# Attention scores with 128 instead of 82 stationary columns, and idle products behind the output projection of each second image

## The reference, cut to what matters

```python
B, N, D = x.shape                       # 32, 164, 192
H, d = (N_HEADS, D_HEAD)                # 12, 16
q = (x @ Wq + bq).reshape(B, N, H, d).transpose(0, 2, 1, 3)
k = (x @ Wk + bk).reshape(B, N, H, d).transpose(0, 2, 1, 3)
scores = jnp.einsum('bhqd,bhkd->bhqk', q, k) * SCALE
allowed = jnp.abs(idx[:, None] - idx[None, :]) <= half      # half = 64
scores = jnp.where(allowed[None, None], scores, -jnp.inf)
```

## Time and profile before

| | |
|---|---|
| median of 3 runs | 2442.05 us (2440.94 to 2452.29) |
| the profiled execution's own time | 2410.74 us |
| its span | 2409.0 us |
| TensorE busy | 2301.1 us, 96% of the span |
| VectorE busy | 1878.0 us, 78% |
| ScalarE busy | 1397.2 us, 58% |
| mean granted clock of TensorE | 0.974 of full speed |

### The profile page before, as it was taken

How to read it: one execution, slowest core, us unless ns; L and a number is a source line. 1 busy time by engine, 2 the same in 40 slices (tenths; PEclk the granted TensorE clock), 3 DMA queues, 4 the chain that set the end, 5 groups by cost and what they waited for, 6 DMA issues and landing times.

```text
span 2409.0 us, 48738 instructions
## 1 busy us (share of the span) xinstructions
PE 2301.1 (96%) x19971; PEld 2153.2 (89%) x19971; DVE 1878.0 (78%) x2364; ACT 1397.2 (58%) x1391; POOL 229.8 (10%) x133
## 2 busy tenths in 40 slices
PE   7699989999999889999999999989999999999999
PEld 6466877777777789999999999989999999999999
DVE  8799755666666487766766767689999999999995
ACT  5689113444444554435435344588888888888881
POOL 5522000000000021211211111000000000000000
PEclk9899997999999899999999999999999999999999
DMA  7655131111111100000000000210000000000000
GB/s 238 178 149 152 47 142 34 45 47 44 47 47 44 37 22 27 20 15 26 20 24 19 19 26 24 90 59 23 24 22 23 23 23 23 23 23 23 23 19 10
DMA packets 99326, 115.82 MB, mean 48 GB/s; under 512 B 15271, under 2 KB 90551, under 8 KB 98487
## 3 DMA queue, kind: packets, MB, share of 16 engines
q1 hardware_dynamic: 79087, 89.38, 12.3%
q10 hardware_dynamic: 16520, 14.34, 2.0%
q0 software_dynamic: 3616, 10.54, 1.7%
HBM read 83.36 MB, written 30.86 MB: 47 GB/s over the span
## 4 chain that ended last, share of the span: by engine, by line
PE 64%; issue 0%; DVE 0%
PE spline_acc L1915 27%; PE spline_acc L1888 10%; PE spline_acc L1887 10%; PE spline_acc L1889 10%; PE spline_acc L1909 5%; PE spline_acc L1911 2%; PE spline_xT L764 0%; DVE spline_f L1664 0%; DVE spline_weights_low L1647 0%; DVE spline_x L1734 0%; DVE spline_x L1737 0%
## 5 line engine op out<-in xcount | busy, mean ns | idle before, releaser
L1915 PE MATMUL spline_acc<-spline_weights,spline_f 128*128 128x192 f32 x3936 | 672.2, 328 | 0.0
L1915 PEld LDWEIGHTS spline_acc<-spline_weights,spline_f 128*128 128x128 f32 x3936 | 637.4, 190 | 0.0
L1887 PE MATMUL spline_acc<-spline_f,spline_weights_high 128*128 128x328 f32 x1536 | 480.5, 313 | 2.5 <-DVE spline_weights_low L1647 2.5
L1888 PE MATMUL spline_acc<-spline_f,spline_weights_high 128*128 128x328 f32 x1536 | 481.2, 313 | 0.0
L1889 PE MATMUL spline_acc<-spline_f,spline_weights_low 128*128 128x328 f32 x1536 | 477.7, 311 | 0.0
L1887 PEld LDWEIGHTS spline_acc<-spline_f,spline_weights_high 128*128 128x128 f32 x1536 | 289.1, 188 | 2.8 <-DVE spline_weights_low L1647 2.8
L1889 PEld LDWEIGHTS spline_acc<-spline_f,spline_weights_low 128*128 128x128 f32 x1536 | 289.3, 188 | 0.0
L1888 PEld LDWEIGHTS spline_acc<-spline_f,spline_weights_high 128*128 128x128 f32 x1536 | 289.3, 188 | 0.0
L1909 PE MATMUL spline_acc<-spline_weights_split,spline_f_high 128*128 128x384 f32 x656 | 218.2, 389 | 8.2 <-issue 8.2
L1664 DVE SCALAR_TENSOR_TENSOR spline_f<-spline_front 128x984 fp32r<-128x984 f32 x128 | 145.6, 1178 | 100.2 <-PE spline_acc L1889 94.9
L1021 DVE TENSOR_REDUCE attend_max<-scores_by_query 82x6 f32<-82x876 f32 x128 | 136.3, 1065 | 57.5 <-PE scores_by_query L1352 56.8
(11 more groups left out here) (229 smaller groups left out, 4266.6 us busy)
## 6 DMA issues: line engine op xcount, KB each, us to landing
spline_front<-pos_scr SPq DMA_DIRECT2D x32, 540.0 KB, 4.4
hid_scr<-spline_hid SPq DMA_DIRECT2D x64, 164.0 KB, 1.8
spline_xn<-hid_scr SPq DMA_DIRECT2D x41, 256.0 KB, 3.1
attend_spread<-rec_scr SPq DMA_DIRECT2D x128, 61.5 KB, 2.1
pix_scr<-spline_front SPq DMA_DIRECT2D x32, 225.0 KB, 3.8
spline_weights_raw<-w SPq DMA_DIRECT2D x1, 6144.0 KB, 21.4
spline_weights<-w SPq DMA_DIRECT2D x4, 1536.0 KB, 6.2
spline_x<-h_scr SPq DMA_DIRECT2D x41, 96.0 KB, 1.9
```

The lines of the kernel that those rows point to most:

```text
L1887: nc.tensor.matmul(z, high, x_high, start=start, stop=False)
L1888: nc.tensor.matmul(z, high, x_low, start=False, stop=False)
L1915: last = nc.tensor.matmul(z, f_rest[i][:, cols], w2[:, i, r, :], start=False, stop=stop)
```

## The change

Two things are done. First, the stationary operand of scores, masks and subtracted maxima is widened from 82 (`ROWS`) to 128 (`P`) columns, and the output with it to 128 partitions of PSUM; partitions 82 to 127 are never read. For this `q1`, `k1` and `k2` become views into tiles `wide` with 46 zeroed columns behind them, `piece` and `pick` are made 128 wide, and POOL zeroes the six tails. Second, `keep_going` is called in each pair but the last, in image 1 in front of part 1, which is behind the output projection: 13 products in the first pair, 4 in the others.

```diff
-        self.piecer = sb("window_piece_r", [P, 2, SPAN], F32R)
+        self.piecer = sb("window_piece_r", [P, 2, WINDOW + P], F32R)
-        self.pickr = sb("attend_pick_r", [P, HG, ROWS], F32R)
+        self.pickr = sb("attend_pick_r", [P, HG, P], F32R)
...
-        q1, k1, k2 = ([sb(f"attend_{k}{u}", [P, HG, PT], F32R) for u in range(2)] for k in ("q1_", "k1_", "k2_"))
+        wide = {k: [sb(f"attend_{k}{u}", [P, HG * PT + P - ROWS], F32R) for u in range(2)] for k in ("q1_", "k1_", "k2_")}
+        q1, k1, k2 = ([y[:, 0:HG * PT].rearrange("p (g n) -> p g n", g=HG) for y in wide[k]] for k in ("q1_", "k1_", "k2_"))
...
+            for y in wide["q1_"] + wide["k1_"] + wide["k2_"]:
+                pool.memset(y[:, HG * PT:].bitcast(F32), 0.0).then_inc(zeros_set, 1)
...
-            pool.wait_ge(zeros_set, 6)
+            pool.wait_ge(zeros_set, 12)
...
+            def columns(k, u, r, g, at):
+
+                at += g * PT
+                return wide[k][u][r, at:at + P]
+
...
-                            nc.tensor.matmul(sc[0:ROWS, j, g * SPAN:(g + 1) * SPAN],
-                                             q1[u][r, g, i * TOK + n * ROWS:i * TOK + (n + 1) * ROWS],
+                            nc.tensor.matmul(sc[:, j, g * SPAN:(g + 1) * SPAN],
+                                             columns("q1_", u, r, g, i * TOK + n * ROWS),
...
-                        last = nc.tensor.matmul(to, piecer[r, n, at:at + ROWS], edge, start=False,
+                        last = nc.tensor.matmul(to, piecer[r, n, at:at + P], edge, start=False,
...
-                            nc.tensor.matmul(tp[0:ROWS, j, g * SPAN:(g + 1) * SPAN],
-                                             k[r, g, i * TOK + c * ROWS:i * TOK + (c + 1) * ROWS],
+                            nc.tensor.matmul(tp[:, j, g * SPAN:(g + 1) * SPAN],
+                                             columns(k, u, r, g, i * TOK + c * ROWS),
...
-                        last = nc.tensor.matmul(tp[0:ROWS, j, g * SPAN:(g + 1) * SPAN], pickr[r, g, :],
+                        last = nc.tensor.matmul(tp[:, j, g * SPAN:(g + 1) * SPAN], pickr[r, g, :],
...
+                        if q == 1 and i == 1 and more:
+                            keep_going(13 if first else 4, xb[:, claim(use(t, V[0])), 0:HG * P])
```

More of the change, by code:

```diff
@@ L142, in stage @@
         self.rest_low = sb("attend_rest_low", [P, 1])
-        self.piece = sb("window_piece", [P, 2, SPAN])
+        self.piece = sb("window_piece", [P, 2, WINDOW + P])
         self.mask = sb("window_mask", [P, 2, EDGE])
-        self.pick = sb("attend_pick", [P, HG, ROWS])
+        self.pick = sb("attend_pick", [P, HG, P])
         self.ones_row = sb("attend_ones_row", [P, PT])
@@ L1000, in _ @@
         def _(dve):
-            dve.wait_ge(zeros_set, 6)
+            dve.wait_ge(zeros_set, 12)
             def norm_in(tt, u):
@@ L1247, in _ @@
                 high(k1[0][:, g, :], start(START["K"][g]))
-            act.wait_ge(zeros_set, 6)
+            act.wait_ge(zeros_set, 12)
             for i in range(2):
@@ L1339, in add_mask @@
                         r = slice(32 * row, 32 * row + 32)
-                        of = scores[0:ROWS, bank, 0:SW].rearrange("p (g n) -> p g n", n=SPAN)
+                        of = scores[:, bank, 0:SW].rearrange("p (g n) -> p g n", n=SPAN)
                         if p < 2:
@@ L1360, in keys_scores @@
                 for g in range(HG):
-                    for k in (k1[u], k2[u]):
+                    for k in ("k1_", "k2_"):
                         for j in range(4):
                             r = slice(32 * j, 32 * j + 32)
-                            nc.tensor.matmul(tp[0:ROWS, j, g * SPAN:(g + 1) * SPAN],
-                                             k[r, g, i * TOK + c * ROWS:i * TOK + (c + 1) * ROWS],
+                            nc.tensor.matmul(tp[:, j, g * SPAN:(g + 1) * SPAN],
+                                             columns(k, u, r, g, i * TOK + c * ROWS),
                                              q1[u][r, g, i * TOK + FROM[c]:i * TOK + FROM[c] + SPAN],
-                                             start=(g == 0 and k is k1[u]), stop=False)
+                                             start=(g == 0 and k == "k1_"), stop=False)
                 add_mask(tp, c, [(j, j) for j in range(4)], False)
@@ L1475, in _ @@
             keep_going(48, tp[:, 0, 0:HG * P])
-            pe.wait_ge(zeros_set, 6)
+            pe.wait_ge(zeros_set, 12)
             for j in range(2):
@@ L2049, in layouts @@
         "wo": wo.reshape(P, HG, D),
-        "pick": np.tile(-(row % DH == group).astype(f32)[..., None], (1, 1, ROWS)),
+        "pick": np.tile(-(row % DH == group).astype(f32)[..., None], (1, 1, P)),
         "minus_low": -np.concatenate([row % 32 >= DH, row % 32 >= DH], 1).astype(f32),
@@ L2054, in layouts @@
         "mask": np.tile(np.where(np.stack([mask, mirror], 1), NEG, 0.0).astype(f32), (4, 1, 1)),
-        "piece": np.tile(np.stack([piece, piece[:, ::-1]], 1).astype(f32), (4, 1, 1)),
+        "piece": np.tile(np.pad(np.stack([piece, piece[:, ::-1]], 1), ((0, 0), (0, 0), (0, P - ROWS))).astype(f32), (4, 1, 1)),
         "patches": x.reshape(B, 3, HS, K, HS, K).transpose(1, 3, 5, 0, 2, 4).reshape(PATCH, B, PIX),
```

## The result

The changed kernel took 2475.76 us (median of 6 runs, 2462.14 to 2486.78), the kernel before 2439.78 us (median of its 6 runs, 2412.88 to 2452.29). The ratio is 1.0176, with a 95% interval from 1.0132 to 1.022: slower, by 43 us as the ratio has it (32 to 54) and 36 us by the medians. The two differ because the ratio leaves out the run of 2452.29 us, which is over 1.5% above the fastest of its kernel and so counts as a slow one. I had forecast 22 us, and 2464 us as the time.

The account below looks back on a forecast made before the run. PE was taken to bound attention, busy 26.8 of 29.2 us a pair. Span 2409.0 + 43.3 (wider sets, idle products) - 21.4 (clock) = 2430.9; by medians 2442.05 + 21.9 = 2464 us, range 2432 to 2488.

Parts of the forecast that it names:

- What bounds the kernel, and the step of a set: Attention: PE bounds it; the load sets the step, 0.109 us a set with 128 columns, 0.036 more than before.
- rival 2: Scores and masks in attention: wide loads don't bound the sets, so the kernel gets faster, 2413 us; chance 0.13.
- What lies beside waits: Attention pairs: of 5.0 us added on PE, waits hide 2.3, leaving 2.7 a pair, 40.5 over 15 pairs.
- The start and the six memsets: Before the first pair: four parts with 36 sets cost 1.3 us; POOL's six memsets are costed at nothing.
- The last pair: Last attention pair: 84 sets and no idle products, 3.0 us, half taken as hidden, so 1.5 us.
- What the clock gives back: Wait behind image 1's output projection: idle products fill it, winning all 21.4 us of four long pairs.
- The carry-over to the median: Whole kernel: the median of runs stands 31.3 us above the profiled execution, and this is carried over.
- Rival 3: Unprofiled runs: their extra 31.3 us is low clock that the change clears too, giving 2433 us; chance 0.15.
- my sum: Whole kernel: forecast of the profiled execution's own time, 2432.6 us, against 2410.74 before the change.
- Rival 1: Attention pairs: the clock isn't helped or falls in more pairs, giving 2485 to 2500 us; chance 0.17.

Follow-up runs that it names:

- wide_only: The changed kernel without its idle products (128 stationary columns only): 2501.88 us, ratio 1.0338 to the kernel before.
- before_again: The kernel before, unchanged, run and profiled once more: 2422.42 us against 2422.35, ratio 1.0025.
- idle_8: The kernel before (82 columns) with idle products, 13 in the first pair and 8 in the others but the last: 2416.14 us, ratio 0.9931.
- wide_idle_2: The changed kernel with 4 more idle products in each pair but the last, in image 1 before part 2: 2472.49 us, ratio 1.0223 to the kernel before.

## Why the prediction was right in its direction and 12 us short

By its own steps:

- **What bounds the kernel, and the step of a set.** Right. A set of 128 columns steps by 0.11 us, the sets by themselves give 29.95 us a pair at 96 columns and 32.05 at 128, and rival 2 (the load doesn't bind) falls, at 32 rows as for the full array of the earlier trace rows. The Trainium skill, "TensorE: Matmul & The Clock Gate", section "LDWEIGHTS (loading the stationary operand)", puts a load at columns / 1.2 ns whatever the rows, 107 ns here as an estimate from that page: at clock 1.00 the trace agrees within 5 ns, at clock 0.50 it shows 0.21 us. The same page's section "Weight-path perf modes — Fast Weight Load (FWL) and DoubleRow" has a faster load that the compiler turns on by itself with 128 columns that are not FP32: for these fp32r loads the trace shows none of it.
- **What lies beside waits.** Nearly. Added on PE some 5.2 rather than 5.0, since four idle products hold PE for 0.94 us and not 0.7; hidden 1.9 rather than 2.3; left 3.3 us a pair rather than 2.7. That the query sets are not hidden was right (2.6 of 2.6 us); of the key sets' 1.7 some 0.7 are hidden where they alone are wide, and 1.0 beside wide query sets (32.5 against 31.8). The idle products add 0.45 us to the pair of wide_only, so half of them lies in what is left of the wait. Over 15 pairs this step was 9 us short.
- **The start and the six memsets.** The first exponential came 7.5 us later (355.84 against 348.29), where I had 1.3. In before_again, with nothing changed, it stands at 357.9, so I don't put the rest down to the change. The memsets cost nothing, as I had it: POOL's wait behind them fell from 6.00 us to 5.35.
- **The last pair.** From its first exponential to the end it is 5.0 us longer (2464.0 - 862.8 against 2409.0 - 812.8 is 1601.2 against 1596.2); the two low stretches there are 34.1 us together, 27.3 before, which is 3.4 of them, and the 84 sets are the 1.5 that I had.
- **What the clock gives back: the term that was mis-sized.** I took all 21.4 us as won, since each low stretch of these pairs began a few us behind the wait that the products fill. In the two profiled executions the fifteen pairs got back 7, which is no more than two profiles of the kernel before differ by. By the runs it is some 9: at an unchanged clock the pairs, the start and the last pair would make 49.5 + 1.3 + 1.5 = 52 us, and the ratio has 43, with an interval of 32 to 54 that just holds 52. The products do work on the clock: with 82 columns they take 24 us off the lost time. But I had costed the width at nothing there, and it isn't: by itself it adds 42 us of lost time, 14 more columns add as much, and what the products take off again (49 us) leaves the change at 66 us, against 68 to 80 for the kernel before in other batches. The term was some two to three times too large, for a reason that my forecast did not have, and that the change won anything on the clock is likely and not shown.
- **The carry-over to the median.** I added 31.3 us between profiled execution and median as a constant. It is no constant: 31 for the kernel before, 10 for the changed one, 6 in before_again, and in wide_only the median lies 13 us below the profiled execution. The runs of one kernel differ by their clock (before: 2401.43 us at 0.979 and 2436.59 at 0.965), and the profile that stood for the kernel before had a better one (0.974) than its runs had on average in any batch (0.967 to 0.972). That accounts for 5 to 17 of the 31 us, since its own lost time is 63 us; for the rest no run shows a cause, as the clocks of the runs behind 2442.05 us are not on record. Rival 3 had that much right; that the change clears these falls too it had wrong.

The errors partly cancel in the medians: the profiled execution was 33.1 us longer than my sum (2465.74 against 2432.6), 9.0 of it from the waits, 14.4 from the clock in the pairs, 6.2 from the start and 3.4 from the clock in the last pair; the carry-over took 21.3 back. That the median came within 12 us is in good part luck. Rival 1 (the clock isn't helped, 2485 to 2500) described the width's side of the matter, though as a failure of the idle products, which it is not: with the same columns they help, by 24 us of lost time at 82 and 49 at 128.

**What stays open.** Why the clock falls in one pair and not in the next, when PE did the same ahead of both, and why in every second pair of wide_only. The runs show that with wider sets the lost time is higher (113 and 115 us against 73) and that with full-array products at the wait it is lower. For such products in the middle of the sets there are one profile and two batches to compare. The falls of the changed kernel are not tied to a wait, as I had read it. What in these sets does it I did not separate; whether products on 32 rows keep the clock up less than full ones was not tested by itself. And for the places of the falls I have one profiled execution of each kernel (two of the kernel before).

## What to carry to other kernels

Where small products change their stationary operand each time, look at its number of columns first: here it set the step (0.073, 0.085 and 0.11 us for 82, 96 and 128), and padding it up to the full array cost time though the moving operand stayed the same. Look at the clock in the stretch around the change, before and after, and over several runs and not one profile: a change that leaves PE busier can still lower it. Fill a wait with idle products only as far as the wait reaches; beyond it each costs PE its time (0.18 us here, 1.05 for a further group of four), and in idle_8 and wide_idle_2 it bought back no more than that.

## What the runs showed of the hardware that I had not expected

- The granted clock fell from 1.00 to 0.50 with PE busy for 3.40 of the 3.40 us ahead (412.3 to 415.7, 583.0 to 586.4), when nearly all it ran were products on 32 rows, and stayed at 1.00 at the same place of other pairs with the same products and the same busy time (485.1 to 488.5).
- The fall came in every second pair of wide_only, seven times running and 71.7 us apart, while in the kernel before the pairs that it hit differed between two executions.
- 96 stationary columns in place of 82 raised the lost time (73 to 113 us) as much as 128 did (115 us), though they add a quarter as much to the pair.
- Four idle products in between two groups of others hold PE for 0.9 us (621.84 to 622.78), though each further one adds 0.18 (0.7 us for four more in idle_8).
